# Three of the four batches of the last expert layer moved into the last units of the attention before it, and its gate taken by an exponential

## What is computed

```python
x = x + _L3_xattn_ref(_layernorm(x), ctx_1024, Wq, bq, Wk, bk, Wv, bv, Wo, bo)
...
    flat = hidden_states.reshape(-1, h)
    routing_scores = jax.nn.relu(flat @ W1 + b1) @ W2 + b2
    gate = jax.nn.sigmoid(jnp.tanh(flat @ Wg1 + bg1) @ Wg2 + bg2)
    routing_scores = routing_scores * gate
    expert_probs = jax.nn.softmax(routing_scores, axis=-1)
    top_idx = jnp.argmax(expert_probs, axis=-1)
    routed = flat * expert_scales[top_idx] + expert_biases[top_idx]
```

## Time and profile before

| | |
|---|---|
| median of three runs | 2943.49 us (2937.85 to 2947.49) |
| the profiled execution, its own time | 2946.27 us |
| its span (first to last instruction, with the last DMA) | 2944.3 us |
| phase 6, units 13, 14 and 15 by the copies that end them (L779) | 2751.3 to 2790.0, to 2830.2, to 2856.9 us |
| last projection of phase 6 | to 2865.4 us |
| phase 7 | 2865.4 to 2944.3 us, 78.9 us |

### The profile page before, as it was taken

One profiled execution on the slowest core, in us unless ns is written; L12 is line 12 of the kernel. 1 busy time (PEld: TensorE's weight loads), 2 busy tenths in 40 slices (PEclk: granted clock), 3 DMA queues, 4 the chain that ended last, 5 costly groups with the idle time before them and its releaser, 6 DMA issues.

```text
span 2944.3 us, 38824 instructions
## 1 busy us (share of the span) xinstructions
PE 2757.4 (94%) x14660; PEld 1398.1 (47%) x14660; DVE 1634.6 (56%) x2980; ACT 1585.0 (54%) x2688; POOL 292.2 (10%) x233
## 2 busy tenths in 40 slices
PE   7999999999899898998899999979989999999988
PEld 3434444443477766776333333267643343434333
DVE  5767777776474454442111221046577777877825
ACT  1677777777300112010677878922237777776762
POOL 2010100100110101111010010022201001010000
PEclk7899999999899998999999999989979999998986
DMA  5432342330300002000734536020043333424200
GB/s 111 68 41 33 52 52 50 45 45 2 92 1 29 0 1 65 1 1 17 131 45 68 66 62 69 5 85 1 12 56 57 45 58 45 63 28 45 24 5 29
DMA packets 68951, 125.51 MB, mean 43 GB/s; under 512 B 20976, under 2 KB 45464, under 8 KB 65312
## 3 DMA queue, kind: packets, MB, share of 16 engines
q1 hardware_dynamic: 67616, 120.61, 26.7%
q10 hardware_dynamic: 1152, 2.44, 0.3%
HBM read 42.47 MB, written 2.10 MB: 15 GB/s over the span
## 4 chain that ended last, share of the span: by engine, by line
PE 56%; DVE 4%; ACT 3%; issue 2%; SPq 2%; DMA 0%; ACTq 0%; POOL 0%; POOLq 0%; DVEq 0%
PE psum L190 35%; PE psum L697 12%; PE psum L1819 6%; DVE mpart L882 2%; ACT probs L762 2%; SPq L992 1%; PE psum L276 1%; PE psum L1812 0%; SPq L993 0%; PE psum L707 0%; DVE prod L1602 0%; PE psum L716 0%; DMA qst<-qp_lo 0%; DVE masked_hi L1906 0%; DVE masked_lo L1907 0%
## 5 line engine op out<-in xcount | busy, mean ns | idle before, releaser
L762 ACT ACTIVATE probs<-psum 128x512 f32<-128x512 f32 (+3 forms) x2080 | 1277.8, 696 | 380.1 <-PE psum L190 378.4
L882 DVE TENSOR_REDUCE mpart<-psum 128x2 f32<-128x804 f32 x1024 | 976.7, 991 | 317.1 <-PE psum L190 308.5
L697 PE MATMUL psum<-probs,vt 128*17 128x512 f32 (+1 forms) x4992 | 668.6, 610 | 2.1 <-ACT probs L762 2.1
L190 PE MATMUL psum<-qst,kst 50*128 50x512 f32 (+3 forms) x2496 | 607.2, 452 | 12.0 <-ACT probs L762 4.9
L190 PEld LDWEIGHTS psum<-qst,kst 50*128 50x128 f32 (+3 forms) x2496 | 269.3, 185 | 416.2 <-issue 255.4
L190 PE MATMUL psum<-kst,qst 48*128 48x402 f32 x2048 | 416.4, 429 | 47.7 <-DVE mpart L882 45.6
L190 PEld LDWEIGHTS psum<-kst,qst 48*128 48x128 f32 x2048 | 199.2, 196 | 356.5 <-issue 182.2
L190 PE MATMUL psum<-wv,ctxT 128*128 128x256 f32 (+1 forms) x624 | 181.1, 419 | 1.5 <-DVE kp_lo L863 0.5
L697 PEld LDWEIGHTS psum<-probs,vt 128*17 128x17 f32 (+1 forms) x4992 | 84.8, 96 | 200.6 <-issue 158.9
L190 PE MATMUL psum<-ctxT,wk 128*128 128x512 f32 (+1 forms) x384 | 157.2, 539 | 22.3 <-DMA ctxT<-in_ctxT 21.3
L190 PEld LDWEIGHTS psum<-wv,ctxT 128*128 128x128 f32 (+1 forms) x624 | 109.6, 194 | 77.7 <-issue 58.6
(11 more groups left out here) (281 smaller groups left out, 2762.5 us busy)
## 6 DMA issues: line engine op xcount, KB each, us to landing
kst<-kp_hi SPq DMA_DIRECT2D x144, 200.1 KB, 5.8
ctxT<-in_ctxT SPq DMA_DIRECT2D x36, 512.0 KB, 5.9
kst<-kp_lo SPq DMA_DIRECT2D x72, 200.1 KB, 5.4
qst<-qp_hi SPq DMA_DIRECT2D x144, 64.0 KB, 4.5
kst<-kp_hi SPq DMA_DIRECT2D x84, 100.1 KB, 2.9
qst<-qp_lo SPq DMA_DIRECT2D x72, 64.0 KB, 5.1
kst<-kp_lo SPq DMA_DIRECT2D x42, 100.1 KB, 3.0
stage<-in_L_ffn_W SPq DMA_DIRECT2D x16, 256.0 KB, 4.5
```

What stands on the lines that cost most here:

```text
L190: last = e.matmul(dst, lhsT, rhs, start=i == 0, stop=i == len(pairs) - 1)
L697: t = e.matmul(c.bank(self.acc)[32 * h:32 * h + VW, :], self.vt[0:kn, kc, self.head(g, h), :], p[0:kn, h % self.wide, :], start=kc == 0, s ...
L762: e.activation(self.probs[n % slots][0:kn, :, :], c.psum[0:kn, k:k + self.wide, :], ACT.Exp if softmax else ACT.Sigmoid, scale=DH ** -0.5) ...
L882: e.tensor_reduce(self.mpart[:, :, p * (SEQ // P) + qt, i], c.psum[:, k:k + 2, 0:MAX_WIDTH], AX.X, ALU.max).then_inc(c.drained(k), 1)
```

## The change

- Phase 7 joins the chain of phases 5 and 6: its weights have a place from phase 5 on, and SP issues its ten loads behind those of phases 5 and 6, before it waits for anything of phase 5's work.
- The attention of phase 6 is handed the expert layer (`after`). Batch b of it, for b = 0, 1, 2, is put into unit 13 + b (`UNITS - 3 + b`), on 18 places at equal distances, three of them empty. Its steps that use PSUM take banks of `misc`. Its `relu`, `tanh`, `hotT` and `h` lie in the place of `ctxT`, one buffer of each instead of two. Engines call `tensor_step`, `scalar_step` and `vector_step` where the list has such a step.
- The normalisations for batches 0, 1 and 2 are put at 5.4 to 6.3, 9.4 to 10.3 and 13.4 to 14.3.
- Phase 7 keeps batch 3 alone: its normalisation and then its steps, one after the other.
- The gate is 1 / (1 + exp(-z - b)): an Exp on ACT with scale -1 and a negated bias (made once by ACT), then an addition of 1 and a reciprocal on DVE.
- The two halves of `f3_hidden` and of `f3_scores` become steps of their own. `make_iota` (POOL) moves to the start of phase 6.

```diff
-CHAINS = ((0,), (1, 2, 3), (4,), (5, 6), (7,))
+CHAINS = ((0,), (1, 2, 3), (4,), (5, 6, 7))
...
+        if self.after:
+            self.after.share(self)
...
-            if b + 1 < BATCH and f < LAST_PHASE:
+            if b + 1 < BATCH and self.after:
+                put(self.norm.steps(f + 1, b), first + GROUPS + 1.4, first + GROUPS + 2.3, misc)
+                put(self.after.batch_steps(b), UNITS - 3 + b + 0.02, UNITS - 2 + b - 0.02, misc)
+            elif b + 1 < BATCH:
                 put(self.norm.steps(f + 1, b), first + GROUPS + 1.9, min(first + GROUPS + 3.2, UNITS - 0.02), misc)
...
+            elif self.after and self.after.owns(step):
+                self.after.tensor_step(e, step)
...
+            self.after.gates.make_iota(e)
...
+    def batch_steps(self, g):
+        f = self.f
+        ready = [("f3_hidden", f, g, 0), ("f3_hidden", f, g, 1), ("f3_scores", f, g, 0), ("f3_scores", f, g, 1),
+                 ("f3_rows", f, g)] + self.gates.softmax_steps(g) + self.gates.largest_steps(g)
+        return ready + [("idle",), ("f3_turn", f, g), ("idle",)] + [("f3_row", f, t) for t in range(4 * g, 4 * g + 4)]
+    def share(self, attention):
+        place, rows = attention.ctxT[:, :, :].rearrange("p k s -> p (k s)"), 4 * DM
+        self.left = ("values", attention.f, BATCH - 1, LAST_KC)
+        self.early = [place[:, i * SEQ:(i + 1) * SEQ] for i in range(2)] + [
+            place[0:E3, 2 * SEQ:3 * SEQ], place[:, 3 * SEQ:3 * SEQ + rows].rearrange("p (t d) -> p t d", d=DM)]
...
-        ring, placed = Ring(*range(8)), []
-        for g in range(BATCH):
-            if g in mine:
-                placed += spread(self.norm.steps(f, g), g - 2, g - 1.2)
-            ready = [("f3_hidden", f, g), ("f3_scores", f, g), ("f3_rows", f, g)] + self.gates.softmax_steps(g)
-            placed += spread(ready + self.gates.largest_steps(g) + [("idle",), ("f3_turn", f, g)], g - 1, g + 0.5)
-            placed += spread([("f3_row", f, t) for t in range(4 * g, 4 * g + 4)], g + 0.6, g + 1.3)
-        self.order = in_order(placed)
...
+        c, f, g = self.c, self.f, BATCH - 1
+        self.late = [c.sbuf(sc, "relu", [P, SEQ])[:, :], c.sbuf(sc, "tanh", [P, SEQ])[:, :], c.sbuf(sc, "hotT", [E3, SEQ])[:, :],
+                     c.sbuf(sc, "h", [P, 4, DM])[:, :, :]]
+        self.order = in_order(spread(self.norm.steps(f, g) + self.batch_steps(g), 0, 1))
+        ring = Ring(*range(8))
+        for step in self.order:
+            c.number(step, ring if step[0] in self.BANKED + ("n_turn",) else None)
...
+    def buffers(self, g):
+        return self.late if g == BATCH - 1 else self.early
+    def wait_place(self, e, g, before):
+        k, v = self.c.at(self.left if g == 0 else before)
+        if g < BATCH - 1:
+            e.wait_ge(self.c.filled(k), v)
...
+            if g == j == 0:
+                self.wait_weights(e)
+                a = c.act.count(e.activation(self.minus_bg2[:, :], self.bg2[:, :], ACT.Copy, scale=-1.0))
+                e.wait_ge(c.act.sem, a)
+            self.wait_place(e, g, ("f3_scores", f, g - 1, j))
...
+        elif kind == "f3_scores" and step[3] == 1:
+            k, v = c.at(step)
+            e.wait_ge(c.filled(k), v)
+            e.activation(self.gate[:, tiles_of(step[2])], c.bank(k)[:, 0:4], ACT.Exp, scale=-1.0,
+                         bias=self.minus_bg2[:, 0:1]).then_inc(c.drained(k), 1)
...
-                e.activation(self.gate[:, tiles_of(step[2])], c.bank(k)[:, 0:4], ACT.Sigmoid,
-                             bias=self.bg2[:, 0:1]).then_inc(c.drained(k), 1)
...
+                a = c.dve.count(e.tensor_scalar(gate, gate, 1.0, None, ALU.add))
+                e.wait_ge(c.dve.sem, a)
+                a = c.dve.count(e.reciprocal(gate, gate))
+                e.wait_ge(c.drained(k0), v0)
+                e.wait_ge(c.dve.sem, a)
+                a = c.dve.count(e.tensor_tensor(rows, rows, over(gate, E3), ALU.mult))
                 gates.last[g] = c.dve.sem, a
...
+        elif kind == "f3_rows":
+            g = step[2]
+            if g == 0:
+                k, v = c.at(self.left)
+                e.wait_ge(c.filled(k), v)
+            elif g < BATCH - 1:
+                e.wait_ge(*x_final(c, f, g - 1))
+            e.wait_ge(*x_final(c, f - 1, g))
...
-                    Attention(c, norm, 6, "L3", True, True), FeedForward3(c, norm, 7)]
+                    Attention(c, norm, 6, "L3", True, True, FeedForward3(c, norm, 7))]
+        self.all.append(self.all[6].after)
```

More of the change, by code:

```diff
@@ L802, in scalar @@
                 e.activation(self.mT[:, :], c.bank(k)[0:MAX_ROWS * 4 * GROUP, 0:P], ACT.Copy).then_inc(c.drained(k), 1)
+            elif self.after and self.after.owns(step):
+                self.after.scalar_step(e, step)
             else:
@@ L934, in vector @@
                 e.tensor_tensor(row, row, c.bank(k)[:, 0:DM], ALU.add).then_inc(c.drained(k), 1)
+            elif self.after and self.after.owns(step):
+                self.after.vector_step(e, step)
             else:
@@ new lines, with owns, tensor_step @@
+    BANKED = ("f3_hidden", "f3_scores", "f3_turn", "f3_row")
+    def buffers(self, g):
[4 more added lines that the diff above has]
+            e.wait_ge(self.c.filled(k), v)
+    def owns(self, step):
+        return step[0][:3] == "f3_" or step[0][:2] == "g_"
+    def tensor_step(self, e, step):
+        c, f, gates, kind = self.c, self.f, self.gates, step[0]
+        if kind in ("f3_hidden", "f3_scores", "f3_row"):
+            k, v = c.at(step)
+            if v > 1:
+                e.wait_ge(c.drained(k), v - 1)
+        if kind == "f3_hidden":
+            _, _, g, j = step
+            if g == j == 0:
+                self.wait_weights(e)
+            if j == 0:
+                e.wait_ge(*self.norm.hT_made(f, g))
+            w = (self.w1, self.wg1)[j]
+            mm(e, c.bank(k), [(w[:, q, :], c.hT[:, q, rows_of(g)]) for q in range(KC)]).then_inc(c.filled(k), 1)
+        elif kind == "f3_scores":
+            _, _, g, j = step
+            k0, v0 = c.at(("f3_hidden", f, g, j))
+            e.wait_ge(c.drained(k0), v0)
+            src, w, n = self.buffers(g)[j], (self.w2, self.wg2)[j], (E3, 1)[j]
+            for i in range(4):
+                t = mm(e, c.bank(k)[:, i * n:(i + 1) * n], [(src[:, i * P:(i + 1) * P], w[:, 0, :])])
+            t.then_inc(c.filled(k), 1)
+        elif kind == "f3_turn":
+            e.wait_ge(c.sem("gates_hot"), c.nth["g_hot", f, step[2]])
+            gates.turn(e, step, gates.hot[0])
+        elif kind == "f3_row":
+            t = step[2]
+            k0, v0 = c.at(("f3_turn", f, t // 4))
+            e.wait_ge(c.drained(k0), v0)
+            mm(e, c.bank(k), [(self.buffers(t // 4)[2][:, t % 4 * P:(t % 4 + 1) * P],
+                               self.scale_bias[:, :, :].rearrange("e a d -> e (a d)"))]).then_inc(c.filled(k), 1)
@@ L2279, in tensor @@
     def tensor(self, e):
-        c, f, gates = self.c, self.f, self.gates
-        self.wait_weights(e)
         for step in self.order:
[L2283 to L2302, removed]
-                t.then_inc(c.filled(k), 1)
-                e.wait_ge(c.drained(kt), vt)
-                for i in range(4):
-                    t = mm(e, c.bank(k2)[:, i:i + 1], [(self.tanh[g % 2][:, i * P:(i + 1) * P], self.wg2[:, 0, :])])
-                t.then_inc(c.filled(k2), 1)
-            elif kind == "f3_turn":
-                e.wait_ge(c.sem("gates_hot"), c.nth["g_hot", f, step[2]])
-                gates.turn(e, step, gates.hot[0])
-            elif kind == "f3_row":
-                t = step[2]
-                k0, v0 = c.at(("f3_turn", f, t // 4))
-                e.wait_ge(c.drained(k0), v0)
-                mm(e, c.bank(k), [(self.hotT[t // 4 % 2][:, t % 4 * P:(t % 4 + 1) * P],
-                                   self.scale_bias[:, :, :].rearrange("e a d -> e (a d)"))]).then_inc(c.filled(k), 1)
-            else:
-                self.norm.tensor(e, step)
@@ L2351, in vector, with vector_step @@
[L2351 to L2360 removed]
+            self.scalar_step(e, step) if self.owns(step) else self.norm.scalar(e, step)
+    def vector_step(self, e, step):
+        c, f, gates, kind = self.c, self.f, self.gates, step[0]
+        if kind == "f3_scores":
+            _, _, g, j = step
+            k, v = c.at(step)
+            ts = tiles_of(g)
+            rows, gate = gates.v[:, ts, :], self.gate[:, ts]
+            if j == 0:
+                if g == 0:
+                    self.wait_weights(e)
```

124 lines of the change are left out of this document (49 added, 75 removed).

## The result

The changed kernel is slower, by 0.8%: 2968.49 us (2962.44 to 2972.99) against 2944.64 (2937.85 to 2947.59) for the kernel before, six executions each, a ratio of 1.008 with a 95% interval of 1.0062 to 1.0099. The forecast was 2923.7 and faster. The profiled execution took 2966.70 us, its span is 2964.6: 20.3 longer than before.

What follows compares the result with a forecast made beforehand. PE, busy 94% of 2944.3 us, was taken as the bound. -44.2 + 14.6 + 4.8 + 6.5 - 1.5 = -19.8 us gave 2926.5 profiled, 2923.7 as median; forecast case 2917 to 2931, whole range 2911 to 2936.

Steps and rivals of the forecast that it cites:

- The tail: Phase 7 after the last addition: 8.9 + 13.75 + 8.65 + 3.4 = 34.7 us where 78.9 stood, 44.2 less.
- what the last units pay: Units 13, 14 and 15 each take one moved batch: +14.6, +4.8 and +6.5 us.
- The gaps: PE's idle time, 3.8 us in unit 14 and 3.0 in unit 15, could take part of a batch's 9.7 us.
- unit 13: Takes batch 0 and most of batch 2's normalisation: +14.6 us, bounds +6.6 and 22.0.
- unit 15: DVE free, ACT no longer the bound: +6.5 us, bounds +5.3 to +9.7.
- Unit 14: Takes batch 1, PE's lower-clock stretch partly given back: +4.8 us, ends -0.3 and +9.7.
- Rival 4: Units 13 and 14: PE's clock falls after gaps between PE and DVE, net +18, 2961 us; chance 0.03.
- The ring of three banks: Units 13 and 14: f3_row products hold banks, stopping PE and DVE's maxima; +12, 2936 us; chance 0.20.
- Units 5, 6, 9 and 10: DVE's normalisation work, 4.7 us, moves into the unit ahead, where PE is the busier: -1.5 us for all four.
- Weight loads at nothing: Ten early loads, 4.5 us of SP's time, cost nothing; the 7.6 us wait at phase 7's start goes.
- The gate: Phase 7, products to hotT: no table load, some 0.1 us sooner; two small DVE operations added; together +0.25 us.
- theory 1: From the experiments: the clock falls because narrow products give TensorE little to do though it counts as busy.

Runs made afterwards that it cites:

- experiment 5: Changed kernel with f3_row on 128 rows and f3_scores on 128 columns: 2942.74 us, ratio 1.0000 to the kernel before; second comparison 1.0004.
- experiment 1: Changed kernel with f3_row products on 128 rows instead of 16: 2946.87 us, ratio 0.9997 to the kernel before; second comparison 1.0018.
- experiment 6: Kernel before, no batch moved, parts added cumulatively: early weights 0.9953, exponential gate 0.9964, f3_row on 128 rows 0.9939, f3_scores on 128 columns 0.9948.

## Why the prediction was wrong

**The tail held.** From the last addition of the last projection to the end it is 34.5 us (2930.12 to 2964.6) where 34.7 was forecast, and part by part: PE's first products of batch 3 began 8.3 us after that addition (2938.43 - 2930.12) where 8.9 was forecast, 14.1 more to `hotT` (13.75), 8.6 for the rows (8.65), 3.45 for the store (3.4). No table load stood there. The -43.0 above is less than -44.2 because the last projection, at a clock of 0.57, took 1.5 us more than before.

```profile
2929.70 0.42 DVE L945 TENSOR_TENSOR x<-x,psum 128x256 f32<-128x256 f32 x1 [0.44 <-PE psum L190]
...
2938.43 3.39 PE L190 MATMUL psum<-hT,w 128*128 128x512 f32 x4 [0.78 <-ACT hT L290]
```

**The step that failed is what the last units pay.** Forecast +14.6 + 4.8 + 6.5 = 25.9 for units 13 to 15; measured 3.9 in unit 12 and 18.5, 18.9 and 17.8 in these, 59.0. It failed twice, in unequal parts, and the kernel of experiment 5 separates them: with the clock kept at 0.95 and more, units 12 to 15 take 45.6 + 50.5 + 50.5 + 34.9 = 181.5 us against 148.3 before, +33.2 (183.0 in its second profile).
- *The clock, 26 us of the 33 missing.* I priced each batch on PE "at the higher clock", 9.7 us, from rows of phase 7 at 1.00, and did not ask whether the moved products would leave the clock there. The signs were in the earlier trace rows: the last `f3_row` products ran at the lower level with PE hardly idle, and PE was busy 8.00 of 8.00 us at 0.51 in unit 14. Of the 26 us, 15 came back with `f3_row` on 128 rows (192.2 us in experiment 1) and 11 only with `f3_scores` on 128 columns, in part in the falls that before has too.
- *The gaps, 7 us.* I let PE's idle time take part of the moved work, and gave 3.9 us of the lower clock in unit 14 back. In the kernel of experiment 5 PE is busy 29.0 us longer in units 12 to 15 (167.6 and 138.6), just what three batches at 9.7 come to, and idle 4.2 longer (13.8 and 9.7): the gaps took nothing. At a high clock unit 13 paid 11.9 and unit 15 8.7, both inside their bounds. Unit 14 paid 10.2, past its upper end of +9.7, although it ran at 0.97 where it had 0.83. And `f3_hidden` of a batch stands ahead of the copy that ends the unit before, so that of batch 0 fell into unit 12 (+2.3), which had no term, and unit 15 held none and paid 8.7 for 6.1 us of work.

**Rival 4 is the one that came, by another mechanism.** It priced the lower clock in units 13 and 14 at 2961 us and let it decide from 55 us at the lower level; 67 us were, 41 of them in these two units. But it put the fall down to gaps between PE and DVE, and the argument against it, more work for PE, was the error: a part of the work that was added keeps PE busy with 16 of 128 rows. The Trainium skill (TensorE: Matmul & The Clock Gate, A second HAM failure mode) speaks of idle times between groups of matmuls; here the clock fell in unit 13 with PE idle for 0.7 us in the 6 us before. In experiment 1 PE is idle for 4.5 us of that unit (50.35 - 45.85) and the clock stays at 1.00, in after for 4.0 (57.06 - 53.06) and it falls. A chance of 0.03 was far too low for a clock that the rows of before already showed at the lower level without a gap.

**The other terms.** *The ring of three banks* (0.20) was to cost 12 us; PE's waits for a row's last addition are 0.7 us in unit 13, and with the clock kept all its added idle time is 4.2. *Units 5, 6, 9 and 10*, -1.5: units 5 and 9 did not move, 6 and 10 each took 43.5 us for 43.0, +1.0 in all. *Weight loads at nothing*: right, and their leaving the path was worth 10.8 us, not 7.6. *The gate*: right that it costs nothing; it gains nothing either.

**A term that was missing: unit 7.** The earlier normalisation of batch 0 took its last steps out of unit 7. First before, then after:

```profile
2485.80:2528.25 42.45, 41.79 (x262) 17.76 (x260) 32.01 (x41) 31.89 (x65) 0.00 (x0) 1.00 0.35 40
2487.41:2532.79 45.38, 44.84 (x258) 18.67 (x257) 31.97 (x41) 31.56 (x63) 0.00 (x0) 0.89 0.36 41
```

It is too regular for chance. In all six profiles of kernels with the earlier normalisations unit 7 takes 45.3 to 47.2 us at a clock of 0.86 to 0.90, in all eight of the others 42.4 to 42.5 at 0.99 or 1.00: 3 to 5 us. What went from its start are four transposes on 128 rows (2485.43 in before), and the clock now falls there, at about 2487.5. It fits theory 1, but no run tests it.

**Why the idea could not win much.** With wide rows, a batch costs 8.7 to 11.9 us in a unit. In phase 7, four batches take 58.4 us with wide rows and one by itself 35.7 (the last window of after, with 16 rows), so three more cost about 23 there, under 8 each, since they overlap. The fastest kernel here, 16.6 us below before, has the early loads and the wide rows and moves no batch.

## What to carry to other kernels

A product on few rows of the array can cost more than its own columns: behind it, the work of others can run at half clock (1.91 us for 1.05), so before moving such products under a busy TensorE, fill the rows (zeros in the stationary operand do) and price both levels. Ask of a moved block not only what its old place gives back but what it costs there when overlapped; here each of the three moved batches cost under 8 us where it stood. And measure the small, separable parts of a change alone: one line of this one, the chain, gave 0.9953 by itself, while the whole gave 1.008. And look for what leaves a unit as well as for what enters it.

## What was not expected of the hardware

- Zeros on 128 rows kept the clock as real data did (ratios 1.0051 and 1.0042), numbers on 16 rows did not (1.0095).
- A wait of 7.6 us cost 10.8 in the profiles, 3.0 of it because products behind it ran at 1.2 GHz.
- Eight table loads of 1.28 us each in phase 7 cost nothing that a median shows (0.9953 with them, 0.9964 without).
- The same unit runs at different clocks in different executions: unit 12, the same in the two kernels of experiment 6 without and with the gate, took 43.3 us at 0.96 and 41.8 at 1.00. Unit 7 fell to 0.86 to 0.90 in every profile once four transposes had left it.
